# A graph layer on one core: gathered rows as f32 matmul operands, the coefficient in the one-hot table

## What is computed

```python
xn = layernorm(x)
# graph part: per edge a message, per (relation, target) a mean, per relation a weight matrix
h = segment_sum(xn[src] * edge_weight, edge_type * N + dst) / max(count, 1)
graph = einsum('rnc,rco->no', h.reshape(R, N, C), weight) + xn @ root + bias
x = x + graph + linear_attention(xn)
x = x + top2_of_6_experts(layernorm(x))   # three 256x256 layers per expert
```

## Time and profile before

| what | value |
|---|---|
| timed runs, median of 3 | 3181.22 us |
| the profiled execution, its span | 3900.9 us |
| first block, node tables | 0 to about 750 us |
| first portions, key sums | about 750 to 930 us |
| loop and last super-tile | 930 to 3901 us |
| matmuls of the row products | 2 x 1666 |

### The profile page before, as it was taken

The page is one execution under the profiler, slowest core; times in us unless marked ns, Lnnn a source line. Parts: engine busy times, 40 slices in busy tenths (PEclk is TensorE's granted clock), DMA queues, the critical chain, the costliest instruction groups (busy, mean ns, idle before and its releaser), DMA issues.

```text
span 3900.9 us, 48061 instructions
## 1 busy us (share of the span) xinstructions
PE 3132.7 (80%) x16807; PEld 2709.1 (69%) x16808; DVE 2360.3 (61%) x5405; ACT 2004.5 (51%) x3996; POOL 1638.6 (42%) x1696
## 2 busy tenths in 40 slices
PE   6999999766878778777777777787787778787788
PEld 5888887656767767666666667676676667677677
DVE  4497552246666667566666656666565666666675
ACT  3555555334555555454555555555555455545564
POOL 0000000145555555554555555554545455555540
PEclk9999999888888888888889888888888889898899
DMA  6665555543233333233323333233323333233320
GB/s 242 250 259 196 210 210 212 224 144 112 84 93 95 99 96 94 82 94 91 90 77 96 95 92 89 85 97 89 92 83 91 90 93 91 79 97 93 100 67 11
DMA packets 179841, 456.72 MB, mean 117 GB/s; under 512 B 46604, under 2 KB 104918, under 8 KB 159405
## 3 DMA queue, kind: packets, MB, share of 16 engines
q0 software_dynamic: 80352, 219.14, 19.5%
q1 hardware_dynamic: 97074, 232.64, 16.5%
q10 hardware_dynamic: 2172, 1.85, 0.1%
HBM read 296.01 MB, written 158.29 MB: 116 GB/s over the span
## 4 chain that ended last, share of the span: by engine, by line
PE 41%; another core or an unknown queue 12%; DVE 10%; ACT 10%; issue 7%; DVEq 1%; DMA 0%; SPq 0%; ACTq 0%
PE bank L1655 27%; PE acc L1709 7%; DVE row_lo L1394 4%; ACT row_hi L1216 4%; ACT bank L1231 3%; ACT h_hi L1230 2%; PE acc L1718 1%; PE bank L1793 1%; PE bank L1682 1%; PE bank L1691 1%; PE acc L1655 1%; DVE y L1540 1%; DVE h_lo L1473 1%; DVE sel L1388 1%
## 5 line engine op out<-in xcount | busy, mean ns | idle before, releaser
L1159 POOL DMA_INDIRECT ring<-y_tab,tab x1666 | 1624.1, 975 | 1401.6 <-PE acc L1709 869.9
L1230 ACT ACTIVATE h_hi<-bank,bias_t 128x512 fp32r<-128x512 f32 (+1 forms) x600 | 408.9, 682 | 1078.1 <-remote 565.1
L1709 PE MATMUL acc<-row_hi,sel 128*128 128x256 f32 x1666 | 501.6, 329 | 446.5 <-DVE row_lo L1394 255.5
L1709 PEld LDWEIGHTS acc<-row_hi,sel 128*128 128x128 f32 x1666 | 369.9, 222 | 508.3 <-DVE row_lo L1394 291.1
L1216 ACT ACTIVATE row_hi<-ring,tab 128x256 fp32r<-128x256 f32 x1666 | 704.1, 510 | 31.4 <-PE acc L1709 19.4
L1394 DVE SCALAR_TENSOR_TENSOR row_lo<-ring,tab,row_hi 128x256 fp32r<-128x256 f32 x1666 | 685.1, 479 | 48.9 <-ACT row_hi L1216 34.4
L1473 DVE TENSOR_TENSOR h_lo<-bank,h_hi 128x512 fp32r<-128x512 f32 (+1 forms) x600 | 392.6, 676 | 447.2 <-ACT bank L1231 360.5
L790 PE MATMUL yb<-wr_hi,xhl 128*128 128x512 f32 x1568 | 510.9, 398 | 31.5 <-ACT yst L351 25.4
L1655 PE MATMUL bank<-ew_hi,h_hi 128*128 128x256 f32 x1176 | 384.2, 327 | 179.0 <-DVE h_lo L1473 177.7
L1709 PE MATMUL acc<-row_lo,sel 128*128 128x256 f32 x1666 | 480.9, 315 | 13.4 <-issue 13.2
L1540 DVE SCALAR_TENSOR_TENSOR y<-bank,gate,y 128x256 f32<-128x256 f32 x490 | 213.0, 479 | 349.7 <-PE bank L1655 227.7
(11 more groups left out here) (272 smaller groups left out, 5219.7 us busy)
## 6 DMA issues: line engine op xcount, KB each, us to landing
y_tab<-yst SPq DMA_DIRECT2D x97, 1024.0 KB, 3.9
ring<-y_tab,tab POOLq DMA_INDIRECT x1666
xt_tab<-xhl SPq DMA_DIRECT2D x25, 1024.0 KB, 3.9
xc<-xt_tab SPq DMA_DIRECT2D x25, 1024.0 KB
x<-x_tab SPq DMA_DIRECT2D x49, 256.0 KB
xs<-in_x SPq DMA_DIRECT2D x24, 512.0 KB, 6.0
x_tab<-xs SPq DMA_DIRECT2D x24, 512.0 KB, 5.0
out<-y SPq DMA_DIRECT2D x24, 512.0 KB
```

The costliest lines, as they stand in the source:

```text
L1159: pool.indirect_dma_start(out=out_ap, out_offset=None, in_=y_tab[:, :], in_offset=bass.IndirectOffsetOnAxis(ap=idx_ap, axis=0)).then_inc(s ...
L1230: act.activation(dest[:, m, 0:W], b[:, 0:W], ACT.Relu, bias=bias)
L1709: last = pe.matmul(sums(t), sel[:, p % BUFS, q, :], half, start=False, stop=False, skip_group_check=True)
```

## The change

The rows go to TensorE as they were gathered, in f32, and the coefficient goes into the one-hot table. VectorE's `prepare` compares a whole portion at once, from `iota_w` in SBUF, into an f32 `sel`; ScalarE's `weigh` multiplies each 128x128 table by the edges' coefficients, in place; `aggregate` makes one matmul per edge tile from `sel` and `ring`, both f32, and waits for `sel_ready` and for the rows themselves. `high`, `one_hot`, `low_rows`, `row_hi` and `row_lo` go. `sel` has four buffers. `ramp`'s PSUM bank becomes a sixth bank of the rotation. Portions are prepared where `READY_AT` says, and on TensorE portion 0 moves ahead of the transposes. What GpSimd and the DMA queues are told to do stays the same.

```diff
-SLOTS, BUFS = 6, 2
+SLOTS, BUFS = 6, 4
...
+READY_AT = {0: (5,), 1: (6,), 2: (7, 8), 3: (9, 10), 4: (11,)}
...
+            ring = sbuf(pc, "ring", [P, SLOTS, PT, C])
             with ExitStack() as px:
-                ring = sbuf(px, "ring", [P, SLOTS, PT, C])
                 xring = sbuf(px, "xring", [P, C])
-            row_lo = sbuf(pc, "row_lo", [P, SLOTS, PT, C], F32R)
             xlo = sbuf(pc, "xlo", [P, C], F32R)
-            row_hi = sbuf(pc, "row_hi", [P, BUFS, PT, C], F32R)
-            sel = sbuf(pc, "sel", [P, BUFS, PT, NT], F32R)
+            sel = sbuf(pc, "sel", [P, BUFS, PT, NT])
...
-            NBANK = 5
+            NBANK = 6
             bank = [psum(pc, f"bank{i}") for i in range(NBANK)]
-
-            ramp = psum(pc, "ramp")
...
-                def high(n, p, first=0, end=PT):
-
-                    if first == 0:
-                        act.wait_ge(tab_in[n % 2], 16 * SUB * (n // 2 + 1))
-                        act.wait_ge(rows_in[p % SLOTS], 16 * gathers(n, p))
-                        act.wait_ge(portion_used, portions_before(n, p) - BUFS + 1)
-                    for q, (t, k) in list(enumerate(tiles_of_portion(p)))[first:end]:
-                        last = act.activation(row_hi[:, p % BUFS, q, :], ring[:, p % SLOTS, q, :],
-                                              ACT.Copy, scale=tab[:, n % 2, t, k, 2:3])
-                    if end == PT:
-                        last.then_inc(hi_ready, 1)
+                def weigh(n, p):
+                    if p >= parts(n):
+                        return
+                    act.wait_ge(hot_ready, PARTS * n + p + 1)
+                    for q, (t, k) in enumerate(tiles_of_portion(p)):
+                        last = act.activation(sel[:, p % BUFS, q, :], sel[:, p % BUFS, q, :], ACT.Copy,
+                                              scale=tab[:, n % 2, t, k, 2:3])
+                    last.then_inc(sel_ready, 1)
...
@@ -1234,24 +1225,23 @@
                     act.activation(std[:, 0:T], mv[:, 0:T, 1], ACT.Sqrt, bias=eps_ln[:, :]).then_inc(std_c, 1)
                     if more:
                         queries(i, plan)
+                        weigh(i + 1, 2)
                     for k in range(KC):
                         act.wait_ge(items_full, full(i, plan, "ft", k))
                         act.activation(ft_hi[:, k, 0:W], bank[plan["ft", k][0]][:, 0:W], ACT.Copy).then_inc(ft_hi_set, 1)
-                    if more:
-                        high(i + 1, 2)
                     b = take(i, plan, "rh", 0)
                     gone(act.activation(rh[:, 0:W], b[:, 0:W], ACT.Relu, bias=bias_t[:, RB1:RB1 + 1]))
+                    if more:
+                        weigh(i + 1, 3)
                     for m in range(KC):
                         hidden("h1", 0, m)
                     if more:
-                        high(i + 1, 3)
+                        weigh(i + 1, 4)
                     act.wait_ge(d_ready, i + 1)
                     act.activation(ex[:, 0:T, :], lg[:, 0:T, :], ACT.Exp).then_inc(ex_ready, 1)
                     for e in range(EXPERTS):
                         for m in range(KC):
                             hidden("h2", e, m)
-                            if more and e in BEHIND_H2 and AHEAD_W3[e] < parts(i + 1):
-                                high(i + 1, AHEAD_W3[e], 3 * m, 3 * m + 3)
                         if e + 1 < EXPERTS:
                             for m in range(KC):
                                 hidden("h1", e + 1, m)
@@ -1260,12 +1250,11 @@
                             act.activation(rw[:, 1, 0:T], gap[:, 0:T], ACT.Exp).then_inc(g2_ready, 1)
                         if e == 1:
                             gone(act.activation(gate_t[:, 0:W], take(i, plan, "gt", 0)[0:8, 0:W], ACT.Copy))
-                        if more and between(e + 1) < parts(i + 1):
-                            high(i + 1, between(e + 1))
-                    if more:
-                        if i + 2 < SUPER:
-                            for p in range(2):
-                                high(i + 2, p)
+                        for p in READY_AT.get(e, ()) if more else ():
+                            weigh(i + 1, p)
+                        if e == EXPERTS - 1 and i + 2 < SUPER:
+                            weigh(i + 2, 0)
+                            weigh(i + 2, 1)
 
...
-                def one_hot(n, p):
+                def prepare(n, p):
+                    if p >= parts(n):
+                        return
                     dve.wait_ge(portion_used, portions_before(n, p) - BUFS + 1)
                     (t, k), size = tiles_of_portion(p)[0], len(tiles_of_portion(p))
-                    dve.tensor_tensor(sel[:, p % BUFS, 0:size, :], ramp[:, 0:P].unsqueeze(1).to_broadcast([P, size, NT]),
-                                      rel_w[:, n % 2, t, k:k + size].unsqueeze(2).to_broadcast([P, size, NT]), ALU.is_equal)
-
-                def low_rows(n, p):
-                    dve.wait_ge(hi_ready, PARTS * n + p + 1)
-                    for q, (t, k) in enumerate(tiles_of_portion(p)):
-                        last = dve.scalar_tensor_tensor(out=row_lo[:, p % SLOTS, q, :], in0=ring[:, p % SLOTS, q, :],
-                                                        scalar=tab[:, n % 2, t, k, 2:3],
-                                                        in1=row_hi[:, p % BUFS, q, :].bitcast(F32),
-                                                        op0=ALU.mult, op1=ALU.subtract)
-                    last.then_inc(lo_ready, 1)
-
-                def prepare(n, p):
-                    one_hot(n, p)
-                    low_rows(n, p)
+                    dve.tensor_tensor(sel[:, p % BUFS, 0:size, :], iota_w[:, :].unsqueeze(1).to_broadcast([P, size, NT]),
+                                      rel_w[:, n % 2, t, k:k + size].unsqueeze(2).to_broadcast([P, size, NT]),
+                                      ALU.is_equal).then_inc(hot_ready, 1)
...
@@ -1485,8 +1460,6 @@
                     for t in range(T):
                         last = dve.bn_aggr(mv[:, t, :], stats[:, t, :])
                     last.then_inc(var_c, 1)
-                    if more:
-                        one_hot(i + 1, 1)
                     dve.wait_ge(std_c, i + 1)
                     dve.reciprocal(rstd[:, 0:T], std[:, 0:T])
                     dve.drain()
@@ -1495,7 +1468,7 @@
                                                  ALU.subtract, ALU.mult)
                     last.then_inc(xn_c, 1)
                     if more:
-                        low_rows(i + 1, 1)
+                        prepare(i + 1, 2)
                         query_features(i, plan)
                     dve.wait_ge(items_full, full(i, plan, "ft", KC - 1))
                     for k in range(KC):
@@ -1503,16 +1476,13 @@
                         gone(dve.tensor_tensor(ft_lo[:, k, 0:W], bank[plan["ft", k][0]][:, 0:W],
                                                ft_hi[:, k, 0:W].bitcast(F32), ALU.subtract))
                     if more:
-                        prepare(i + 1, 2)
+                        prepare(i + 1, 3)
                     low("h1", 0)
                     logits(i, plan)
                     if more:
-                        prepare(i + 1, 3)
+                        prepare(i + 1, 4)
                     for e in range(EXPERTS):
-                        second = AHEAD_W3[e] if more and e in BEHIND_H2 and AHEAD_W3[e] < parts(i + 1) else None
-                        low("h2", e, second)
-                        if second is not None:
-                            low_rows(i + 1, second)
+                        low("h2", e)
                         if e == 0:
                             best_two(i, plan)
                         low("h1", e + 1)
@@ -1522,19 +1492,16 @@
                             denominators(i, plan)
                         if more and e == 2:
                             attention(i, plan)
-                        if more and e == EXPERTS - 1:
-                            if i + 2 < SUPER:
-                                prepare(i + 2, 0)
-                        coming = between(e + 1) if more and between(e + 1) < parts(i + 1) else None
-                        if coming is not None:
-                            one_hot(i + 1, coming)
+                        for p in READY_AT.get(e, ()) if more else ():
+                            prepare(i + 1, p)
+                        if e == EXPERTS - 1 and i + 2 < SUPER:
+                            prepare(i + 2, 0)
+                            prepare(i + 2, 1)
...
                 def aggregate(n, p):
 
-                    pe.wait_ge(lo_ready, PARTS * n + p + 1)
+                    if p >= parts(n):
+                        return
+                    pe.wait_ge(sel_ready, PARTS * n + p + 1)
+                    pe.wait_ge(rows_in[p % SLOTS], 16 * gathers(n, p))
                     for q, (t, k) in enumerate(tiles_of_portion(p)):
```

(39 more changed lines are left out.)

3 lines of the change are left out of this document (1 added, 2 removed).

## The result

The changed kernel takes 3280.9 us (median of 4 runs, 3279.5 to 3284.5) against 3181.4 us: a ratio of 1.0318, 95% interval 1.0302 to 1.0334. That is inside the range of rival (a), which had a chance of 0.06.

What follows compares the result with a forecast made beforehand. TensorE was taken to bound the loop, 83.5 of 92.0 us per iteration. 3181 + 275 (f32 matmuls) + 20 (low clock) - 85 (waits) - 5 (first stage) = 3386, written 3385 us; range 3300 to 3480 us.

Steps and rivals of the forecast that it cites:

- rival (a): TensorE's loop runs almost gapless, all the room won back, beat near 95 us: 3224 to 3300 us, chance 0.06.
- (c): TensorE's 446 us of idling before the row products is real and goes, making the kernel faster: 3010 us, chance 0.02.
- (d): The f32 row matmul runs as one record of 0.204 us, making the kernel faster: 3040 us, chance 0.03.
- The f32 price: TensorE's row products: one f32 matmul at 0.409 us replaces two fp32r at 0.236, adding 275 us over 1598 tiles.
- I take 40%, -85 us: Waits in TensorE's loop: 40% of the 204 us of room is won back, -85 us.
- The room: TensorE's waiting and low clock in the timed loop: at most 8.5 us per iteration, 204 us in all.
- the chain over three engines: Hidden to output in each expert stays a cross-engine chain, a reason to count only 40% of the room.
- the 20 us set aside for it: Extra cost for the part of TensorE's added matmul work that meets the low clock: +20 us.
- the sixth bank: An added PSUM bank loosens the rotation, counted among the things that win back waits; no size of its own.
- I take these to be the price of being profiled: Some 740 us of unknown-releaser and issue stalls in the first profile's loop, held absent from timed runs.
- The first stage: The first 68 tiles: 12 us more for TensorE, 28 us less for VectorE; -5 us, between -28 and +15.
- The lower end of the range: The forecast's 3300 us, with 150 us of waits won back at most; the range had 0.80.

Runs made afterwards that it cites:

- e7: The changed kernel with each edge tile's f32 matmul made twice: 3964 us, one run.
- e1: The kernel before, unchanged, profiled a second time: span 3186.2 us, beat 93.4 us; timed at 3181 us.
- e6: The kernel before without VectorE's low rows, TensorE using the rounded rows twice; order, two buffers and five banks kept: 2974 us, ratio 0.9357.
- e3: The kernel before, own order and buffers, with one f32 matmul per edge tile; VectorE still computes the unread low rows: 3343 us, ratio 1.0505.
- e5: The kernel before with six PSUM banks instead of five, the one-hot compare reading its numbers from SBUF: 3181 us, ratio 0.9999.
- e2: The changed kernel with two fp32r matmuls per edge tile on the same rounded operands instead of one f32 matmul: 3041 us, ratio 0.9559.
- e12: e2 with the one-hot compare reading its numbers from PSUM and five banks again: 3041 us, ratio 0.9576 to the kernel before.
- e4: The changed kernel's order and six banks with the kernel before's split rows, two fp32r matmuls per tile and two buffers: 3316 us, ratio 1.0421.
- e9: The kernel before with portions 6, 8 and 10 in f32 without low rows, the other nine split: 3111 us, ratio 0.9784.
- e13: The kernel before, its order, without low rows and with one fp32r matmul per edge tile: 2956 us, ratio 0.9302.

## Why the prediction was right and wrong

**The sign and the dearer matmul were right.** TensorE bounds the loop, one f32 matmul is dearer than two in fp32r, and the two records per instruction cost what they cost in the closing products. Rivals (c) and (d) fell: (c) because the idling behind it shrank to 119.1 us, (d) by e7. The time is that of rival (a), but the beat is 97.7 us and not near 95, because the start was 93.4 us and not 92.0 and the matmul a little dearer.

**The f32 price** was 0.409 us; e7 measured 0.418. Over 1598 tiles that is 290 us in place of 275. The Trainium skill (FP8 and Floating Point Precision, TensorE Precision Notes) has four passes for true FP32, which makes 427 ns at 2.4 GHz by an estimate from that page. The measured 418 ns lies between that and the 409 ns of the closing products, 2% below the estimate.

**The step that failed is "I take 40%, -85 us"** for the waits. The room was sized well, 204 us in the prediction against 24 x 8.1 = 194 us by e1 and e6, in part by luck: the iteration (92.0, measured 93.4 us) and TensorE's own work in it (83.5, measured 85.3 us in e6) were both put too low, and the errors nearly cancel. But nearly the whole of it was won back. With 93.4 us before and 12.1 us of added work an iteration would have taken 105.5 us; it takes 97.7, so 7.8 us went, 187 us in the loop. What the prediction had left standing were the chain over three engines and the low clock. Neither kept its cost. The chain is covered once VectorE's 2.5 us blocks of low rows are out of it (e6: all 8.1 us, the order and the number of matmuls unchanged), and mostly even with them in it once a portion lasts about 2.5 us instead of 1.4 (e3: 99.7 us against a floor of 85.3 + 12.1 = 97.4, so 5.8 of 8.1 us covered). The change does both, and how its 7.8 us divide between the two can't be told, since either alone would win most of them. The low clock followed the idling: 0.97 in e1, 1.00 in e6, 0.99 after, and the 20 us set aside for it were not due either. Of what the prediction counted among the winners, the sixth bank did nothing (e5), and the changed order with its earlier preparation cost time wherever the products were cheap (e2 and e12 against e6, e4 against e1). Four buffers in place of two were not tried alone.

**The odd trace.** "I take these to be the price of being profiled" was wrong as a reason, and with it the remark that the stalls follow bursts of many short records: e1 has the same records and not the stalls. What made that one execution odd stays open. The conclusion that the timed loop lacks those stalls was right. Its damage was small: the loop began at 900.9 us and not at 930.5, so the iteration was 93.4 and not 92.0 us. The first stage won 900.9 - 894.3 = 6.6 us, forecast as 5.

The sum with the measured terms: 3181 + 290 - 187 - 7 = 3277 us, against 3281 measured. That is no independent proof, since the 187 us were read from the changed kernel's own beat. The lower end of the range came from a chosen 150 us of waits won back in its own case, when the profile had no row that kept the last 50 us.

## What to carry to other kernels

When an engine bounds a loop with little idling, ask of every remaining wait what holds it up, and if the change removes exactly that, count the engine's own work as the new beat; lengthening the engine's own blocks covers waits too. Here a dearer form of an operation paid at the few places with late inputs (e9), while the same exchange everywhere lost. And when a span differs from the timed runs by a fifth, take a second trace before building on the first.

## What the runs showed of the hardware

An f32 matmul of 128x128 by 128x256 costs 0.418 us, 3.5 times the 0.118 us of one in fp32r, and one instruction leaves two records of it.

Not expected: the mean length of a gather on GpSimd goes with what VectorE reads. It is 986 ns before (e1), 1029 ns when the compare's source moves from PSUM to SBUF (e5), and 954 or 955 ns where VectorE has no row work left and the compare reads PSUM (e6, e12, e13). The closest pair is e2 and e12, which differ in that source and the number of PSUM banks:

```profile
L1153 POOL DMA_INDIRECT ring<-y_tab,tab x1666 | 1647.7, 989 | 532.5 <-issue 495.7
```

```profile
L1154 POOL DMA_INDIRECT ring<-y_tab,tab x1666 | 1589.4, 954 | 577.7 <-issue 493.0
```

The Trainium skill (SBUF — State Buffer, SBUF: two separate sides) tells of a port pair shared by VectorE and GpSimd, which a VectorE instruction with two SBUF inputs locks against a GpSimd operation that reads SBUF. The direction of these lengths agrees with it, if a gather is such an operation; nothing here shows the lock itself.
